# Fused transformer block on one core: three buffers for the split probabilities, and a head's output folded by TensorE

## The reference

```
h = modulate(layernorm(x), shift_msa, scale_msa)
q, k, v = split(h @ W_qkv + b_qkv)                 # 16 heads of 36
attn = softmax((q * 36**-0.5) @ k.T)               # 512 x 512 for each head
o = attn @ v
x = x + gate_msa * (o @ W_proj + b_proj)
...                                                # the MLP
v = silu(cond) @ W.T + b                           # entries of a skew 64 x 64 matrix A
x = x + ((x @ U) @ expm(A) - x @ U) @ U.T          # U from the QR of P
```

## Time and profile before

| | us |
|---|---|
| median of 3 runs (2688.56 to 2693.1) | 2692.27 |
| the profiled execution | 2695.13 |
| span of its instructions | 2693.5 |
| PE busy | 2381.8 (88%) |
| DVE busy | 1433.2 (53%) |
| ACT busy | 1097.7 (41%) |
| POOL busy | 772.7 (29%) |

### The profile page before, as it was taken

The page is one execution under the profiler, slowest core; times in us unless marked ns, Lnnn a source line. Parts: engine busy times, 40 slices in busy tenths (PEclk is TensorE's granted clock), DMA queues, the critical chain, the costliest instruction groups (busy, mean ns, idle before and its releaser), DMA issues. The chain is left out here.

```text
span 2693.5 us, 48930 instructions
## 1 busy us (share of the span) xinstructions
PE 2381.8 (88%) x15081; PEld 2048.1 (76%) x15081; DVE 1433.2 (53%) x2978; ACT 1097.7 (41%) x2362; POOL 772.7 (29%) x1547
## 2 busy tenths in 40 slices
PE   5698988988989789798998467999999999999998
PEld 1465766756767567576675457999999999999998
DVE  3577676676776766767766473333333333333332
ACT  1265555555555555555655122222222222222221
POOL 1043343343444344334445481111111111111110
PEclk9799989989989899898998688999999999999998
DMA  7122122231222222212221141010101010110100
GB/s 224 43 75 78 54 80 66 63 96 43 86 72 58 76 67 68 89 54 74 75 66 55 62 122 50 27 43 27 39 27 39 27 38 28 38 36 30 36 25 27
DMA packets 90196, 160.52 MB, mean 60 GB/s; under 512 B 22832, under 2 KB 34176, under 8 KB 89920
## 3 DMA queue, kind: packets, MB, share of 16 engines
q1 hardware_dynamic: 77056, 110.35, 14.2%
q0 software_dynamic: 11856, 46.60, 5.3%
q10 hardware_dynamic: 1024, 0.26, 0.0%
HBM read 80.10 MB, written 20.16 MB: 37 GB/s over the span
## 5 line engine op out<-in xcount | busy, mean ns | idle before, releaser
L1649 PE MATMUL bank<-h2T,w 128*128 128x256 f32 x4032 | 531.1, 283 | 9.3 <-issue 6.5
L1649 PEld LDWEIGHTS bank<-h2T,w 128*128 128x128 f32 x4032 | 508.0, 191 | 10.9 <-issue 7.6
L1558 DVE TENSOR_TENSOR glo<-bank,ghi 128x256 fp32r<-128x256 f32 x288 | 122.3, 425 | 688.2 <-ACT bank L1525 688.2
L1662 PE MATMUL bank<-w,ghi 128*128 128x288 f32 x2304 | 476.5, 298 | 0.4
L1524 ACT ACTIVATE ghi<-bank,b 128x256 fp32r<-128x256 f32 x288 | 137.1, 476 | 687.9 <-PE bank L1649 687.8
L869 DVE TENSOR_TENSOR plo<-pf,phi 128x512 fp32r<-128x512 f32 x512 | 365.3, 713 | 87.5 <-ACT pf L738 82.5
L735 ACT ACTIVATE phi<-bank 128x512 fp32r<-128x512 f32 x512 | 303.1, 592 | 252.0 <-PE bank L1049 226.5
L862 DVE TENSOR_REDUCE negm<-bank 128x1 f32<-128x512 f32 x512 | 349.5, 683 | 101.4 <-PE bank L1021 87.7
L1662 PEld LDWEIGHTS bank<-w,ghi 128*128 128x128 f32 x2304 | 367.2, 189 | 2.5 <-DVE x2T L1568 2.0
L1662 PE MATMUL bank<-w,glo 128*128 128x288 f32 x1152 | 340.8, 296 | 0.0
L738 ACT ACTIVATE pf<-bank 128x512 f32<-128x512 f32 x512 | 303.2, 592 | 0.0
(11 more groups left out here) (222 smaller groups left out, 3226.3 us busy)
## 6 DMA issues: line engine op xcount, KB each, us to landing
xln<-x POOLq DMA_DIRECT2D x16, 1152.0 KB, 6.8
qs<-qkhi SPq DMA_DIRECT2D x192, 72.0 KB
ks<-qkhi SPq DMA_DIRECT2D x192, 72.0 KB
wst<-w_fc POOLq DMA_DIRECT2D x34, 288.0 KB, 3.0
x_d<-xln POOLq DMA_DIRECT2D x32, 288.0 KB, 2.5
xa<-x_d SPq DMA_DIRECT2D x32, 288.0 KB, 2.8
xs<-x_d SPq DMA_DIRECT2D x16, 576.0 KB, 3.8
out<-xs SPq DMA_DIRECT2D x16, 576.0 KB, 2.9
```

The source lines that it names most:

```text
L1649: mm = pe.matmul(F[ft % 2][:, 0:CH], w1[0:rows, w, ft * PAR:(ft + 1) * PAR], h[0:rows, a, :], start=(i == 0), stop=(i == len(FULL_PASSES) ...
L1662: mm = pe.matmul(Y[2 * tt + half][:, 0:HALF], g[ft % 2][:, span], w2[:, ft, w, half * HALF:(half + 1) * HALF], start=(ft == 0 and i == 0), ...
```

## The change

1. phi and plo have three buffers in place of two. `PBUF` gives the buffer of each slot (n % 3, but for the last four slots: 0, 1, 2, 1) and `PBUF_BEFORE` the slot that used it last; ACT and DVE wait for the products of that slot, mostly n - 3. pf still has two.
2. `transpose_o` multiplies each tile of `ots` by a constant matrix `fold` (73 x 37) in place of transposing it. Column d of fold picks row d and row 37 + d, column 36 picks the sums. So the high and low parts are added in PE, and `X` has 38 columns a tile.
3. DVE multiplies by the reciprocals right out of PSUM into `early` or `oo`; `oraw`, the reduce and POOL's `divide` are gone, and the semaphore `o_read` becomes `o_norm`.
4. `rv` has four units a batch item (slots 10, 18, 30, 56) of five matmuls each, and `wrot` half the columns, so half the bytes a load.
5. Room: `mrow` lies in free partitions of `ots`, `scaled` in free columns of `carry`.
6. For the second batch item POOL waits for an `ln` unit before it asks for x.

```
@@
-(61, ("v", 0, 3)), (10, ("rv", 0)), (33, ("rv", 1))]
+(61, ("v", 0, 3)), (10, ("rv", 0)), (18, ("rv", 1)), (30, ("rv", 2)), (56, ("rv", 3))]
+RV = 4
...
+PBUF = [_n % 3 for _n in range(SLOTS - 4)] + [0, 1, 2, 1]
+PBUF_BEFORE = [next(_n - _d for _d in range(1, SLOTS) if PBUF[(_n - _d) % SLOTS] == PBUF[_n]) for _n in range(SLOTS)]
...
+        phi = [sb(acts, f"phi{i}", [PAR, TOKENS], fp32r) for i in range(3)]
+        plo = [sb(acts, f"plo{i}", [PAR, TOKENS], fp32r) for i in range(3)]
+        ots_full = [sb(acts, f"ots{i}", [PAR, TOKENS]) for i in range(2)]
+        ots = [ots_full[i][0:2 * HD + 1, :] for i in range(2)]
+        mrow = [ots_full[i][96:96 + TT, 0:PAR].bitcast(fp32r) for i in range(2)]
+        fold = sb(acts, "fold", [2 * HD + 1, HD + 1])
...
-        OW = 2 * HD + 2
+        OW = HD + 2
...
-                    cols = bass.ds((2 * b + i) * (2 * PAR), 2 * PAR)
+                    cols = bass.ds((RV * b + i) * PAR, PAR)
...
-                    if n % TT == 3 and is_there(b, n - TT):
-                        divide(b, n)
...
-                    if is_there(b, n - 2):
-                        act.wait_ge(pv, b * SLOTS + n - 1)
-                    act.activation(phi[n % 2][:, :], S[n % 2][:, :], ACT.Exp, scale=SCALE).then_inc(exp_hi, 1)
+                    if is_there(b, PBUF_BEFORE[n]):
+                        act.wait_ge(pv, b * SLOTS + PBUF_BEFORE[n] + 1)
+                    act.activation(phi[PBUF[n]][:, :], S[n % 2][:, :], ACT.Exp, scale=SCALE).then_inc(exp_hi, 1)
...
+                rows = ident[0:2 * HD + 1, :]
+                dve.tensor_tensor(fold[:, 0:HD], rows[:, 0:HD], rows[:, HD + 1:2 * HD + 1], ALU.add).then_inc(fixed, 1)
+                dve.tensor_copy(fold[:, HD:HD + 1], rows[:, HD:HD + 1]).then_inc(fixed, 1)
...
-                    dve.tensor_reduce(oraw[i][:, :, :], pair, AX.X, ALU.add).then_inc(o_read, 1)
+                    dve.tensor_tensor(head, view[:, :, 0:HD], recip[i][:, :].unsqueeze(2).to_broadcast([PAR, TT, HD]), ALU.mult).then_inc(o_norm, 1)
...
-                    for k in range(2):
-                        for t in range(KT + 1):
-                            mm = pe.matmul(G[g_bank(it, u)][:, k * BATCH:(k + 1) * BATCH], wrot[:, t, k * PAR:(k + 1) * PAR], siluT[:, t, :],
-                                           start=(t == 0), stop=(t == KT))
+                    for t in range(KT + 1):
+                        mm = pe.matmul(G[g_bank(it, u)][:, 0:BATCH], wrot[:, t, :], siluT[:, t, :], start=(t == 0), stop=(t == KT))
...
-                        mm = pe.transpose(X[:, qt * OW:qt * OW + 2 * HD + 1], ots[i][:, qt * PAR:(qt + 1) * PAR],
-                                          ident[0:2 * HD + 1, 0:2 * HD + 1])
+                        mm = pe.matmul(X[:, qt * OW:qt * OW + HD + 1], ots[i][:, qt * PAR:(qt + 1) * PAR], fold[:, :], start=True, stop=True)
```

More of the change, by code:

```diff
@@ L418, in build @@
         negm = [sb(acts, f"negm{i}", [PAR, TT]) for i in range(2)]
-        mrow = [sb(acts, f"mrow{i}", [TT, PAR], fp32r) for i in range(2)]
         pf = [sb(acts, f"pf{i}", [PAR, TOKENS]) for i in range(2)]
-        phi = [sb(acts, f"phi{i}", [PAR, TOKENS], fp32r) for i in range(2)]
-        plo = [sb(acts, f"plo{i}", [PAR, TOKENS], fp32r) for i in range(2)]
-        ots = [sb(acts, f"ots{i}", [2 * HD + 1, TOKENS]) for i in range(2)]
+        phi = [sb(acts, f"phi{i}", [PAR, TOKENS], fp32r) for i in range(3)]
[3 more added lines that the diff above has]
+        mrow = [ots_full[i][96:96 + TT, 0:PAR].bitcast(fp32r) for i in range(2)]
         recip = [sb(acts, f"recip{i}", [PAR, TT]) for i in range(2)]
-        oraw = [sb(acts, f"oraw{i}", [PAR, TT, HD]) for i in range(2)]
+        fold = sb(acts, "fold", [2 * HD + 1, HD + 1])
         early = sb(acts, "early", [PAR, TT, EARLY * HD])
@@ L434, in build @@
         lower = sb(acts, "lower", [RANK, HEADS])
-        scaled = sb(acts, "scaled", [RANK, 2 * RANK])
-        wrot = sb(acts, "wrot", [PAR, KT + 1, 2 * PAR])
+        scaled = carry[0:RANK, BLOCKS * BATCH:BLOCKS * BATCH + 2 * RANK]
+        wrot = sb(acts, "wrot", [PAR, KT + 1, PAR])
         small = sb(acts, "small", [RANK, 7])
@@ L440, in build @@
         G, M, S, O = PB[0:2], PB[2:4], PB[4:6], PB[6]
-        OW = 2 * HD + 2
+        OW = HD + 2
         X, XM, XA = PB[7][:, 0:TT * OW], PB[7][0:TT, 0:PAR], PB[7][:, :].rearrange("p (f t) -> p f t", t=PAR)
-        CONSTANTS = RING + 5
+        CONSTANTS = RING + 7
         modulated, hT_hi = sem("modulated"), sem("hT_hi")
@@ L528, in slot @@
                     for _, i in [u for u in units(b, ENDS_AT.get(n - 2, [])) if u[0] == "rv"]:
-                        if not isinstance(b, int) or 2 * b + i + 1 < 2 * BATCH:
+                        if not isinstance(b, int) or RV * b + i + 1 < RV * BATCH:
                             sp.wait_ge(g_full, g_use(b, ("rv", i)) + 1)
                             alone(sp)
-                            load_wrot(b + (i + 1) // 2, (i + 1) % 2)
+                            load_wrot(b + (i + 1) // RV, (i + 1) % RV)
                     for _, t in [u for u in units(b, ENDS_AT[n]) if u[0] == "qk"]:
@@ L553, in _ @@
                 pool.sem_inc(xo_done, 2)
-                pool.sem_inc(o_norm, 2)
                 pool.sem_inc(row_ready, 1)
@@ L635, in load_next_x @@
                         pool.wait_ge(x1_out, 16 * TT * (b - 1))
+                    if isinstance(b, int) and b == 1:
+                        pool.wait_ge(g_full, g_use(-1, ("ln", KT)) + 1)
                     load_x(pool, b)
@@ L647, in load_residual @@
                     pool.dma_start(gate[:, :], ada_d[bass.ds(b, 1), 2 * C:3 * C].partition_broadcast(PAR)).then_inc(gate_in, 16)
[L649 to L661, removed]
                 def add_x(b, it, qt):
@@ L799, in _ @@
                 dve.sem_inc(m_read, 2)
-                dve.sem_inc(o_read, 1)
+                dve.sem_inc(o_norm, 2)
                 def modulate(it, f):
@@ L854, in take_rotation @@
                     dve.wait_ge(g_full, g_use(it, u) + 1)
-                    dve.tensor_copy(vT[:, bass.ds((2 * it + i) * 2, 2), :],
-                                    G[g_bank(it, u)][:, 0:2 * BATCH].rearrange("p (k b) -> p k b", b=BATCH)).then_inc(g_free, 1)
+                    dve.tensor_copy(vT[:, bass.ds(RV * it + i, 1), :],
+                                    G[g_bank(it, u)][:, 0:BATCH].unsqueeze(1)).then_inc(g_free, 1)
                 def row_max(b, m):
@@ L866, in p_los @@
                     dve.wait_ge(exp_hi, b * SLOTS + n + 1)
-                    if is_there(b, n - 2):
-                        dve.wait_ge(pv, b * SLOTS + n - 1)
-                    dve.tensor_tensor(plo[n % 2][:, :], pf[n % 2][:, :], f32(phi[n % 2][:, :]), ALU.subtract).then_inc(p_lo, 1)
+                    if is_there(b, PBUF_BEFORE[n]):
+                        dve.wait_ge(pv, b * SLOTS + PBUF_BEFORE[n] + 1)
+                    dve.tensor_tensor(plo[PBUF[n]][:, :], pf[n % 2][:, :], f32(phi[PBUF[n]][:, :]), ALU.subtract).then_inc(p_lo, 1)
                 def read_o(b, n):
@@ L875, in read_o @@
                     dve.wait_ge(oT, ho + 3)
-                    dve.wait_ge(o_norm, ho + 1)
                     dve.reciprocal(recip[i][:, :], view[:, :, HD]).then_inc(recip_done, 1)
-                    pair = view[:, :, 0:2 * (HD + 1)].rearrange("p t (two d) -> p t d two", two=2)[:, :, 0:HD, :]
+                    h = (n // TT - 1) % HEADS
+                    if h < EARLY:
+                        if h == 0 and (not isinstance(b, int) or b >= 1):
+                            dve.wait_ge(early_moved, b)
+                        head = early[:, :, h * HD:(h + 1) * HD]
+                    else:
+                        if h == EARLY and (not isinstance(b, int) or b >= 1):
+                            dve.wait_ge(g_full, g_use(b, ("tr", TT - 1)) + 1)
+                        head = oo[:, :, h * HD:(h + 1) * HD]
                     dve.wait_ge(recip_done, ho + 1)
-                    dve.tensor_reduce(oraw[i][:, :, :], pair, AX.X, ALU.add).then_inc(o_read, 1)
+                    dve.tensor_tensor(head, view[:, :, 0:HD], recip[i][:, :].unsqueeze(2).to_broadcast([PAR, TT, HD]), ALU.mult).then_inc(o_norm, 1)
                 def slot(b, n, phase):
@@ L964, in transpose_out @@
                         pe.wait_ge(early_moved, it)
-                    pe.wait_ge(o_read, it * HEADS + (TR_SLOT[qt] // TT + 1 if is_there(it, 0) else 1))
+                    pe.wait_ge(o_norm, it * HEADS + (TR_SLOT[qt] // TT + 2 if is_there(it, 0) else 2))
                     if is_there(it, TR_SLOT[qt] + 5):
@@ L1027, in transpose_max @@
                     if is_there(b, TT * (h - 3)):
-                        pe.wait_ge(o_read, b * HEADS + h - 1)
+                        pe.wait_ge(o_norm, b * HEADS + h)
                     pe.transpose(XM, negm[h % 2][:, :], ident[:, :]).then_inc(mT, 1)
@@ L1047, in values @@
                     v = vv[:, kt, h, 0:2 * HD + 1]
```

(6 more changed lines are left out.)

4 lines of the change are left out of this document (2 added, 2 removed), and 2 rows, old and new, of the table FIRST_SLOT.

## The result

| | before | after |
|---|---|---|
| median of the runs compared (4 each) | 2692.68 | 2730.99 |
| the profiled execution | 2695.13 | 2727.25 |
| ratio of after to before, 95% interval | | 1.0139, 1.0125 to 1.0153 |

What follows compares the result with a forecast made beforehand. PE (TensorE) sets the pace in most slots, busy 153.2 of a steady batch's 174.3 us; +46 -3 -1 -3 +2 +1 -5 = +37 on the median 2692.3 gives 2729 us, range 2700 to 2765.

Steps and rivals of the forecast that it cites:

- Fold, +46: Matmuls by fold at L1061 cost 0.62 us more a head than transposes; partly hidden by waits, +46 us in all.
- DVE and POOL, -4: DVE's shorter read and POOL's lost division give -3 us before slot 40 and -1 among the layer-norm slots.
- Third buffer, -3: Three buffers for phi and plo let ACT start a slot earlier, shortening PE's waits: -3 us, bounds 0 and -15.
- Rotation +2: Five rotation matmuls each at slots 10, 18, 30, 56 instead of ten at 10 and 33: +2 us.
- share of bandwidth +1: The weight load for slot 56 goes out inside x's transfer and may delay x: 0.2 us a batch, +1.
- clock -5: In slots 9 to 11, the halved rotation makes the fall to 1.2 GHz rarer: -5 us, bounds 0 and -9.
- Hardly hidden: Rival: PE's small waits move along with the fold, so 8.5 of 9.9 us a batch shows; 2752 to 2777; chance 0.14.
- Cheap fold: Rival: the fold costs 0.2 us a head if loads go ahead under the previous product; 2690 to 2700; chance 0.12.
- Third buffer decouples: Rival: PE's waits for qklo and hT shrink too, -30 us in all, 2675 with cheap fold; chance 0.10.
- Clock: Rival: matmuls keep 2.4 GHz through slots 9 to 11, shorten half-clock stretches behind slot 40 and loop edge; 2710; chance 0.12.
- ACT's wait: Sign in the profile after: ACT's wait on L1049 for phi falls from 214.9 us to well under 100.
- slot 40's wait: Sign in the profile after: PE's wait for POOL at slot 40 hardly changes in its end.

Runs made afterwards that it cites:

- e1: The kernel before with only a head's four transposes written as plain fp32 matmuls by the identity (73 columns): 1.0130 against before, +36.1 us.
- e2: The kernel after with two buffers for phi and plo and two rotation units at slots 10 and 33: 1.0178 against before, +47.1 us.
- e10: e2 with the division back on POOL, DVE only copying the folded head to oraw: 1.0150 against before.
- e5: The kernel after with two buffers for phi and plo, all else as changed: 1.0136 against before.
- e8: The kernel after with the transposes back (DVE reduces into the head's place, POOL multiplies there) and two buffers: 0.9959 against before.
- e3: The kernel before with the rotation in four units at slots 10, 18, 30, 56 and POOL's wait for the second item's x: 0.9966, -9.0 us.

## Why the prediction was right, by its steps

The forecast, 2729, was met by 2731, but not every term of the sum was: the main mechanism was right, and that the hit is so close is luck.

- **Fold, +46.** Right, and the term that decided. The group was forecast at 0.88 us and took 0.81 at the full level, 0.60 more than the transposes. e1's stage is 31.2 us longer in the table, with 6.4 us of gain in slots 9 to 11 and some 10 in slots 0 to 8 inside it, so about 48 of fold (an estimate). The hiding was drawn wrongly in detail: in e1, slots 12 to 29 took 8.7 us for 40 folds, since those at 17, 21 and 29 vanished whole in waits, which I had counted as less than half hidden; 41 and 45, where I had 1.0 us hidden, took 1.4 each, at half the clock. I had priced every fold at the full level, though the earlier trace rows show 0.50 behind slot 40. The two errors nearly cancel.
- **DVE and POOL, -4.** Not borne out: e2 less e1 is +11. The two differ in the form of the fold and the place of `mrow` too, so the +11 is not the price of DVE and POOL alone; e2 less e10, which differ only in who divides, is +5.5 with intervals that touch. DVE's read did shrink as said, but the 3 us that it was to give in the stretch up to slot 40 are not there (254.0 in e2, 251.3 in e1, 254.1 in e10). The sum had no term for a lower clock in slots 0 to 8 and 41 to 48, where 11.8 us of the difference to e1 lie.
- **Third buffer, -3.** 0 by e5 and e8, within some 3 us. PE's own waits for pf and plo were small, as said, and a lack of buffers made next to none of them. Over 80 to 1500 us they are, before and after:

```profile
PE bank L1048 <- DVE plo L869: 25.3, 33, 2.3
...
PE bank L1037 <- ACT pf L738: 13.2, 25, 3.0
```

```profile
PE bank L1047 <- DVE plo L863: 26.1, 35, 2.3
...
PE bank L1036 <- ACT pf L729: 14.3, 14, 2.9
```

- **Rotation +2, share of bandwidth +1, clock -5.** Together -2, measured -9.0 by e3. The mis-sized terms are two of the rotation's, in the table of stretches: slot 56, which I had at 0.9 us a batch and which took 0.8 in all when it stood alone, and the stretch to slot 40, where I let what leaves 33 and what comes to 30 cancel in the steady batches, and which gave 2.4 there. The clock gave 6.1 for the 5 forecast. x did not land later for the load in its middle (6.2 us in the median for 6.8), and no wait at the rotation for its weights stands in the list after.
- **The terms together.** e2 and e3 add up to +38.1, and after is +38.3: with the third buffer at 0, nothing else is needed. By single runs +46 was +36 (the clock's gain included), -4 was +11, -3 was 0 and -2 was -9. These misses of 3 to 15 us cancel; without that luck the hit within 2 us would not be there.
- **Rivals.** Hardly hidden: not so, in e1 five of a steady batch's 16 folds show with 0.1 us or less (17, 21, 29, 57, 61), the stretch to slot 40 absorbs two more (33, 37), and the one at 9 shows with 0.3. That at 49, which I had counted among the hidden, shows with 0.5 in slots 49 and 50. Cheap fold: out by e1 and by the 0.81. Third buffer decouples: out by e5 and e8; qklo and hT are waited for as long as before. Clock: the part in slots 9 to 11 came in e1, but e3 gave as much with transposes. The half-clock stretch behind slot 40 did not go and made its folds dearer. Behind the loop's edge, in the kernel after, it went in batch 2 (slots 0 to 8 at a granted 1.00 for 0.88) and stayed in batches 3 to 6 (0.88).

- **What the profile was to show.** The 1024 instructions, the read of 0.3 us, ACT's wait far under 100 on the products of the values (11.5), slot 40's wait and the steady batch (180.8 in 178 to 182) came as said. PE is 49 us busier and not 60. And DVE's wait for x did not grow by 1 to 1.5 us a batch: 1.30 in batch 3 for 1.73, in this view of DVE's waits after (5.6 in six waits before):

```profile
DVE stats L249 <- DMA xln<-x: 7.0, 6, 1.4
```

## To carry to other kernels

Before a transpose gives way to a matmul that does more, count instructions and weight loads and not columns: a plain fp32 matmul is two of each, and here that turned a saved multiply on an engine with time to spare into some 40 us on the one that sets the pace. A helper's long wait is worth only what PE waits for that helper, here at most some 2 us a batch beside ACT's 27. Work can stand nearly free in a stretch that a transfer closes, if its own load is asked for early enough: at slot 38 the stretch grew by 0.3 us in all, at slot 35 the kernel by 47.5.

## What the runs showed that was not expected

- The granted clock in slots 9 to 11 rose both with more instructions (e1: 11.5 us at 1.00, where batches 1 and 5 had 14.4 before) and with fewer (e3: 10.1), so the two gains, 6.4 and 6.1 us, don't add up: both edits together gave 7.3 (13.7 less the 8.8 of the half unit, plus the fold's 2.4).
- At the same 119 instructions the granted clock of slots 0 to 8 was 0.94 in one kernel and 0.83 in another, 3.1 us in one batch, with DVE and POOL the less loaded in the slower. Why is open.
- A group of eight fp32 loads and matmuls with 73 rows and 128 weight columns takes 0.81 us at the full level, with 37 moving columns as with 73, and 1.56 at the low one. With 8 moving columns and 128 rows (L1007) eight would be 0.89 us, at the 0.11 us each of the earlier trace rows: fewer moving columns save nothing.
